# Moving the weight sums of down's last chunk and the second group's dots on VectorE, in an octonion FFN with attention shortcut

## The chip, the cores and the metric

The kernel runs on one core of a Trainium2 chip. The metric is the device time of one execution in microseconds (us); lower is better. A core has engines with queues of their own: TensorE (PE in the profile, its weight loads PEld), VectorE (DVE), ScalarE (ACT), GpSimd (POOL), and SyncE (SP), which here only issues DMAs. Each engine runs its queue in order and meets the others through semaphores.

## The reference, cut to what matters

```python
x = L0_attn_x                                   # (1, 2048, 1024), f32
xn = _layernorm(x, axis=-1)
x = x + _L0_attn_ref(xn) + _L0_ffn_ref(xn, w_gate, w_up, w_down)

# _L0_attn_ref: autocorrelation of each row by FFT, its 6 largest lags, softmax, weighted sum of shifted rows
# _L0_ffn_ref, eight components i, j, k of an octonion, S its +-1 product table:
scale = jnp.mean(jnp.abs(W))
Wq = scale * jnp.clip(jnp.round(W / scale), -1.0, 1.0)      # ternary weights
M = jnp.einsum('jik,jod->koid', S_OCT, Wq)
linear(xp, W) = jnp.einsum('...id,koid->...ko', xp, M)
h = silu(linear(xp, w_gate)) * linear(xp, w_up)             # hidden: 8 x 341 or so
out = linear(hp, w_down)
```

The kernel replaces the attention part by the normalised row itself as long as a bound shows that lag zero has all of the softmax's weight. For that bound it needs of each row the spectrum and one number, the dot product of the row's first half with its second. A flag sends rows for which the bound fails to a slow path, which isn't taken here.

## The kernel before, in words

The 2048 rows go in eight groups of 256 (G = 8, two tiles t of 128 rows each). The hidden width of a component (341 units) is cut into three chunks c. For each group there are units of work, each with a bank pair of the accumulator in PSUM: X (transposes of the normalised rows), F (spectrum for the bound), G and U (gate and up of one chunk and one parity Y), L and H (the narrow third chunk, gate and up together), N (down, one tile of rows).

The octonion product is done by a fast form: sums and differences of components on the inputs ("hx" to "hs" and "hop" for the hidden values, x to "xop") and of the weights ("slots"), matmuls on these, and adds of quarters on VectorE behind them.

Who does what to the hidden values of a unit numbered m: ScalarE makes silu of the gate into hx; VectorE multiplies by up (`product`, L1540) and raises h_done; GpSimd waits for h_done, makes four sums (L1975, L1976, L1980, L1981, 128x512 f32, hs_done after each of the last two) and then two low halves (L1985, L1988); ScalarE makes the high halves (`h_high` L1015, `h_sums_high` L1025, which waits for the four sums); TensorE then uses hop for down.

The weights are prepared in the opening, T(m, c) for m = gate, up, down: TensorE transposes them, ScalarE takes signs (L900), VectorE makes the ternary values (`ternary`, L1349, two instructions) and the sums in `weight_slots` (two instructions L1366 and L1367 into a temporary, four more L1374 into the weights). For down the temporary, the ternary values (in zx) and the result wd are f16 in SBUF. GpSimd's sums read and write SBUF too.

The order on each engine is a list written out by hand. The opening ends on VectorE with `ternary(("T", 2, 1))`, `product(("U", 0, 1, 0))`, `weight_slots(("T", 2, 1))`, `out_scales()` (three tiny instructions, L1333 to L1335); second_group follows with `product(("U", 0, 1, 1))`, the adds of L(0,0,0), `least(("F", 1))`, the adds of L(0,0,1) and so on. ScalarE's list at the same place is

```python
            h_high(0, 1, 0)                 # end of the opening
            power(("F", 1))                 # L964, waits for TensorE's spectrum
            h_sums_high(0, 1, 0)            # L1025, waits for GpSimd's four sums of U(0, 1, 0)
            odd_two(("L", 0, 0, 0))         # L947
            eights(("T", 1, 0))             # L928
            refine(2)                       # L842 to L854
            odd_two(("L", 0, 0, 1))         # L947
```

`odd_two` copies half of a unit's sums out of PSUM, and VectorE's `first_adds` (L1423 to L1427) and `second_adds` (L1453 to L1459) of the same unit need that copy. TensorE's order in this stretch: direct products of U(0,1,1), spectrum F(1), first half of L(0,0,0), lags of F(1), first halves of L(0,0,1), L(0,1,0) and L(1,0,1), second half of L(0,0,0), then the second half of L(0,0,1), which waits for the end of that unit's `second_adds`.

A `dot(g, t)` is one VectorE instruction (L1382, 128x512 f32, both inputs in SBUF) with a read of the accumulator. For the second group (g = 1) both stand behind `x_sums_low(("X", 1, 0))`. SyncE's `load_x(2)` overwrites the rows in xr and waits for both dots and for the transposes of X(1,1). Its loads of zx wait for the last `weight_slots`, whose input lies in the same room.

Of the kernel before, what the change touches and what calls it, by code (L numbers as in the profile page):

```python
def octonion_ffn_attention_kernel(nc, x, w_gate, w_up, w_down, dft, lag, out):
# [19 lines left out]
    T = 256  # L21
    NT = T // P
# [94 lines left out]

    place = {u: n for n, u in enumerate(units)}
    bank = [b for _, b in opening] + [(n - OPEN + 3) % 4 for n in range(OPEN, N)]

    owner = {u: ([units[i] for i in range(n - 1, -1, -1) if bank[i] == bank[n] and units[i][0] != "-"] + [None])[0] for n, u in enumerate(units)}

    def is_direct(u):
        return u[0] in "GU" and u[1] == 0 and u[2] < DIRECTS
# [14 lines left out]
    def hidden(u):  # L139
        return (u[1], u[2], u[3]) if u[0] in "GU" else (u[1], 2, u[2])  # L140
# [20 lines left out]
    for u in units:  # L161
        if u[0] in "UH" and hidden(u)[0:2] not in halves and hidden(u)[0:2] != (G - 1, 1):
            two = sorted(spare[:2])
            spare = spare[2:]
            halves[hidden(u)[0:2]] = tuple(i for i, _ in two)
            free_after[hidden(u)[0:2]] = [n for _, n in two if n]
        if u[0] == "N":
            spare += [(halves[u[1], c][u[2]], u) for c in range(NC) if (u[1], c) in halves]
# [7 lines left out]
    with ctx:  # L176
# [76 lines left out]
        def bank_pair(n, rows=P):  # L253
            return acc[0:rows, bank[n], :, :]
# [26 lines left out]
        def slots(m, c):  # L281
            return (wg, wu)[m][:, c, :, :] if c < 2 else wl[:, :, m, 0:REST]
# [1020 lines left out]
        def _(dve):  # L1303
# [9 lines left out]
            def thresholds(m, u):  # L1313
                dve.wait_ge(total_mm, m + 1)
                nc.vector.tensor_reduce(tot[:, m:m + 1], acc[:, bank[place[u]], 0, 0:4], AX.X, ALU.add).then_inc(total_read, 1)
                dve.wait_ge(total_read, m + 1)
                nc.vector.tensor_scalar_mul(thr[:, m:m + 1], tot[:, m:m + 1], 0.5 / N_W).then_inc(thr_done[m], 1)
                dve.wait_ge(thr_done[m], 1)
# [13 lines left out]
            def out_scales():  # L1332
                link(nc.vector.tensor_scalar(osc[:, :], thr[:, 0:1], thr[:, 1:2], 2.0 / HS, ALU.mult, ALU.mult))  # L1333
                link(nc.vector.tensor_tensor(osc[:, :], osc[:, :], thr[:, 2:3], ALU.mult))
                link(nc.vector.tensor_scalar_mul(nosc[:, :], osc[:, :], -1.0))  # L1335

            def weights_of(u):

                _, m, c = u
                rows, cols = (P, WIDE[c]) if m < 2 else (WIDE[c], DB)  # L1340
                return rows, cols, slots(m, c)[:, 2 * NJ:3 * NJ, :] if m < 2 else wt[t_no[u] % 2][0:rows, :, 0:cols]

            def ternary(u):
                _, m, c = u
                k, n = t_no[u], place[u]
                rows, cols, val = weights_of(u)
                for b in range(2):
                    dve.wait_ge(sign_done, 2 * k + b + 1)
                    nc.vector.scalar_tensor_tensor(val[:, 4 * b:4 * b + 4, :],  # L1349
                                                   acc[0:rows, bank[n], b, :].rearrange("p (j d) -> p j d", j=4)[:, :, 0:cols],  # L1350
                                                   thr[0:rows, m:m + 1], wt[k % 2][0:rows, 4 * b:4 * b + 4, 0:cols], ALU.is_gt, ALU.min).then_inc(tern_done, 1)

            def weight_slots(u):
                _, m, c = u
                i = slots_no[u]
                rows, cols, val = weights_of(u)
                dve.wait_ge(tern_done, 2 * t_no[u] + 2)
                two = val.rearrange("p (b i v) d -> p b i v d", b=2, i=2)
                s = tt[i % 2][0:rows, :, :, 0:cols]
                if u == ("T", 1, 0):  # L1360

                    dve.wait_ge(first_slots, 1)
                if u == ("T", 2, 1):

                    dve.wait_ge(term_mm, prod_no["G", 0, 1, 1] + 1)
                nc.vector.tensor_tensor(s[:, 0:3:2, :, :], two[:, :, 0, :, :], two[:, :, 1, :, :], ALU.add)  # L1366
                nc.vector.tensor_tensor(s[:, 1:4:2, :, :], two[:, :, 0, :, :], two[:, :, 1, :, :], ALU.subtract).then_inc(pairs_done, 1)  # L1367
                dve.wait_ge(pairs_done, i + 1)
                for op, (a, alu) in enumerate(((0, ALU.add), (0, ALU.subtract), (1, ALU.add), (1, ALU.subtract))):
                    if m < 2:  # L1370
                        dst = slots(m, c)[:, 4 * op:4 * op + 4, :].rearrange("p (b v) d -> p b v d", b=2)
                    else:
                        dst = wd[0:rows, 4 * op:4 * op + 4, c, :].rearrange("p (b v) d -> p b v d", b=2)
                    last = nc.vector.tensor_tensor(dst, s[:, a:a + 1, :, :].broadcast_to([rows, 2, 2, cols]), s[:, 2:4, :, :], alu)  # L1374
                last.then_inc(slots_done, 1)

            def dot(g, t):
                k = NT * g + t
                dve.wait_ge(norm_done, NT * g + NT)
                if k:  # L1380
                    dve.wait_ge(dot_done, k)
                nc.vector.scalar_tensor_tensor(dj[:, :], xr[:, t, 0:D // 2], 1.0, xr[:, t, D // 2:D], ALU.mult, ALU.mult,  # L1382
                                               accum_out=dots[:, k:k + 1]).then_inc(dot_done, 1)
# [133 lines left out]
            def x_low(u):  # L1517
                four = bank_pair(place[u]).rearrange("p b (i t) -> p (b i) t", t=T)
                at = 4 * u[2]
                dve.wait_ge(xhi_done, x_no[u] + 1)  # L1520
                nc.vector.scalar_tensor_tensor(xop[:, u[1] % 2, at:at + 4, 1, :], four, XS, xop[:, u[1] % 2, at:at + 4, 0, :], ALU.mult, ALU.subtract).then_inc(xlo_done, 1)

            def x_adds(u):
                first_adds(u)
                if u[2] == 1:
                    fold_sum(u)
                second_adds(u)

            def x_sums_low(u):
                at = NJ + 4 * u[2]  # L1530
                dve.wait_ge(xhs_done, x_no[u] + 1)
                nc.vector.tensor_tensor(xop[:, u[1] % 2, at:at + 4, 1, :], bank_pair(place[u]).rearrange("p b (i t) -> p (b i) t", t=T),
                                        xop[:, u[1] % 2, at:at + 4, 0, :], ALU.subtract).then_inc(x_ready, 1)

            def product(u):
                m = h_no[hidden(u)]
                dve.wait_ge(term_mm, prod_no[u] + 1)
                dve.wait_ge(silu_done, g_no["G", *u[1:]] + 1)
                scale = ((hsc4, nhsc4) if is_direct(u) else (hsc, nhsc))[u[3]]
                nc.vector.scalar_tensor_tensor(hx[:, m % 4, :, :], hx[:, m % 4, :, :], scale[:, :],  # L1540
                                               bank_pair(place[u]).rearrange("p b (i t) -> p (b i) t", t=T), ALU.mult, ALU.mult).then_inc(h_done, 1)
# [6 lines left out]
            def least(u):  # L1548
                dve.wait_ge(lag_mm, f_no[u] + 1)
                nc.vector.tensor_reduce(dmin[:, NT * u[1]:NT * u[1] + NT], acc[:, bank[place[u]], 1, :].rearrange("p (t l) -> p t l", t=NT),  # L1550
                                        AX.X, ALU.min).then_inc(bound_done, 1)
# [59 lines left out]
            x_sums_low(("X", 0, 0))  # L1611
            x_sums_low(("X", 0, 1))
            dot(0, 0)
            dot(0, 1)
            thresholds(1, ("U", 0, 0, 0))
            ternary(("T", 1, 0))
# [8 lines left out]
            weight_slots(("T", 0, 1))  # L1625
            least(("F", 0))
            thresholds(2, ("F", 0))
            ternary(("T", 1, 1))
            product(("U", 0, 0, 1))
            x_low(("X", 1, 0))  # L1630
            x_adds(("X", 1, 0))
            ternary(("T", 2, 2))
            x_sums_low(("X", 1, 0))
            dot(1, 0)
            dot(1, 1)
            x_low(("X", 1, 1))
            x_adds(("X", 1, 1))
            ternary(("T", 2, 0))
# [3 lines left out]
            weight_slots(("T", 2, 2))  # L1642
            weight_slots(("T", 2, 0))
            ternary(("T", 2, 1))
            product(("U", 0, 1, 0))
            weight_slots(("T", 2, 1))
            out_scales()

            def second_group():
# [374 lines left out]
```

## Time and profile before

| | |
|---|---|
| median of 3 runs | 553.96 us (553.83 to 554.98) |
| profiled execution, its own time | 553.78 us |
| its span in the trace | 552.0 us |
| TensorE busy | 539.7 us (98%) |
| VectorE busy | 472.3 us (86%) |
| ScalarE busy | 385.0 us (70%) |
| GpSimd busy | 466.7 us (85%) |
| TensorE's granted clock | 1.00 of full speed, in every slice |

The span starts with the first instruction in the trace; 1.78 us of the profiled execution lie outside it. A matmul's end is modelled, so busy time says whether TensorE had work in hand and not how well it was used. Time zero in all the rows is the start of the span.

### The profile page before, as it was taken

The numbers are of one execution on the slowest core, as the hardware profiler recorded it, in microseconds if no ns is written. First come the engines' busy times: TensorE is split into PE (matmuls) and PEld (weight loads), VectorE is DVE, ScalarE is ACT, GpSimd is POOL, SyncE is SP. The second block draws the span as 40 slices with busy tenths as digits, with TensorE's granted clock in tenths as the row PEclk, the third lists the DMA queues.
The fourth block names the chain that finished last, engine by engine and source line by source line (L and its number), as shares of the span: only waits on it lengthen the run. The fifth ranks groups of instructions, "written<-read, shape, count | busy, mean of one in ns | idle before, by whom it ended". The sixth has DMA issues, their size and how long they took to land.

```text
span 552.0 us, 16462 instructions
## 1 busy us (share of the span) xinstructions
PE 539.7 (98%) x6596; PEld 507.2 (92%) x6596; DVE 472.3 (86%) x1227; ACT 385.0 (70%) x622; POOL 466.7 (85%) x337
## 2 busy tenths in 40 slices
PE   6999999999999999999999999999999999999997
PEld 5899998899998999999999999999999999998997
DVE  4987999898888879988998979987998979984965
ACT  4879889976947589665977589766967575646432
POOL 3506739998999998999989998999989999999950
PEclk9999999999999999999999999999999999999999
DMA  9820212013220042201330042201330021302122
GB/s 207 193 78 1 77 27 82 8 38 110 79 88 17 3 153 66 66 1 39 137 100 12 1 152 67 65 4 44 130 99 12 3 77 35 95 3 71 33 87 97
DMA packets 26996, 36.65 MB, mean 66 GB/s; under 512 B 13686, under 2 KB 20774, under 8 KB 26918
## 3 DMA queue, kind: packets, MB, share of 16 engines
q1 hardware_dynamic: 26918, 35.58, 21.8%
q8 instruction: 52, 0.85, 0.6%
q14 instruction: 26, 0.21, 0.1%
HBM read 21.23 MB, written 8.39 MB: 54 GB/s over the span
## 4 chain that ended last, share of the span: by engine, by line
PE 70%; POOL 13%; issue 9%; DVE 4%; DMA 2%; ACT 2%; SPq 0%; POOLq 0%; ACTq 0%; DVEq 0%
PE acc L659 17%; PE acc L495 14%; PE acc L488 13%; PE acc L505 10%; PE acc L649 6%; PE acc L544 4%; POOL hop L1988 3%; POOL hs L1981 3%; POOL hs L1976 3%; POOL hs L1980 3%; PE acc L518 2%; DMA hop<-in_w_gate 2%; PE acc L561 2%; POOL hop L1985 1%; POOL hs L1975 1%
## 5 line engine op out<-in xcount | busy, mean ns | idle before, releaser
L659 PE MATMUL acc<-wd,hop 128*128 128x128 f16 x1920 | 112.7, 219 | 0.8 <-DVE acc L1441 0.4
L659 PEld LDWEIGHTS acc<-wd,hop 128*128 128x128 f16 x1920 | 109.4, 98 | 1.7 <-DVE acc L1441 0.9
L947 ACT ACTIVATE pk<-acc 128x512 f32<-128x512 f32 (+1 forms) x120 | 65.9, 556 | 64.0 <-PE acc L488 26.2
L1988 POOL TENSOR_TENSOR hop<-hs,hop 128x1024 f16<-128x1024 f32 (+1 forms) x46 | 98.2, 2135 | 9.0 <-ACT hop L1025 8.8
L1985 POOL TENSOR_TENSOR hop<-hx,hop 128x1024 f16<-128x1024 f32 (+1 forms) x46 | 98.3, 2137 | 5.3 <-ACT hop L1015 5.3
L505 PE MATMUL acc<-wl,xop 128*128 128x172 f16 x1024 | 84.2, 237 | 1.1 <-DVE acc L1459 0.9
L505 PEld LDWEIGHTS acc<-wl,xop 128*128 128x128 f16 x1024 | 77.6, 97 | 3.2 <-DVE acc L1459 1.1
L1975 POOL TENSOR_TENSOR hs<-hx 128x512 f32<-128x512 f32 (+1 forms) x47 | 60.2, 1281 | 15.3 <-DVE hx L1540 11.7
L1423 DVE TENSOR_TENSOR bd<-acc,pk 128x256 f32<-128x256 f32 (+1 forms) x104 | 41.0, 394 | 30.0 <-ACT pk L947 29.6
L1025 ACT ACTIVATE hop<-hs 128x1024 f16<-128x1024 f32 (+1 forms) x46 | 48.4, 1053 | 23.8 <-POOL hs L1981 23.7
L1980 POOL TENSOR_TENSOR hs<-hs 128x512 f32<-128x512 f32 (+1 forms) x47 | 59.8, 1273 | 3.7
L1981 POOL TENSOR_TENSOR hs<-hs 128x512 f32<-128x512 f32 (+1 forms) x47 | 60.4, 1285 | 0.0
L1976 POOL TENSOR_TENSOR hs<-hx 128x512 f32<-128x512 f32 (+1 forms) x47 | 60.0, 1277 | 0.0
L495 PE MATMUL acc<-xop,wu 128*128 128x256 f16 x448 | 53.3, 273 | 0.0
L488 PE MATMUL acc<-xop,wg 128*128 128x256 f16 x448 | 53.3, 273 | 0.0
L1015 ACT ACTIVATE hop<-hx 128x1024 f16<-128x1024 f32 (+1 forms) x46 | 48.5, 1055 | 6.8 <-DVE hx L1540 3.5
L488 PE MATMUL acc<-xop,wu 128*128 128x256 f16 x448 | 52.3, 273 | 0.5 <-ACT hx L979 0.5
L495 PE MATMUL acc<-xop,wg 128*128 128x256 f16 x448 | 52.7, 273 | 0.0
L488 PEld LDWEIGHTS acc<-xop,wu 128*128 128x128 f16 x448 | 43.6, 98 | 5.6 <-ACT hx L979 0.8
L649 PE MATMUL acc<-wd,hop 85*128 85x128 f16 (+2 forms) x720 | 48.5, 219 | 0.0
L488 PEld LDWEIGHTS acc<-xop,wg 128*128 128x128 f16 x448 | 43.7, 98 | 4.9
L495 PEld LDWEIGHTS acc<-xop,wg 128*128 128x128 f16 x448 | 43.3, 98 | 4.8
(206 smaller groups left out, 1164.2 us busy)
## 6 DMA issues: line engine op xcount, KB each, us to landing
xr<-in_x SPq DMA_DIRECT2D x16, 512.0 KB, 4.4
zx<-in_x SPq DMA_DIRECT2D x16, 512.0 KB, 3.6
out_y<-zx SPq DMA_DIRECT2D x15, 512.0 KB, 2.6
hop<-hop SPq DMA_DIRECT2D x40, 84.0 KB
hop<-hop SPq DMA_DIRECT2D x96, 21.0 KB
hop<-in_w_gate SPq DMA_DIRECT2D x2, 480.0 KB, 9.6
hop<-in_w_up SPq DMA_DIRECT2D x1, 960.0 KB
hop<-in_w_down SPq DMA_DIRECT2D x1, 960.0 KB, 17.3
```

The costliest lines, as they stand in the source:

```text
L488: last = nc.tensor.matmul(acc[:, bank[n], s // 2, T * (s % 2):T * (s % 2 + 1)], wm[:, c, slot, :], xop[:, g % 2, form, level, :], start=s ...
L495: last = nc.tensor.matmul(acc[:, bank[n], s // 2, T * (s % 2):T * (s % 2 + 1)], wm[:, c, slot, :], xop[:, g % 2, form, level, :], start=Fa ...
L505: last = nc.tensor.matmul(acc[:, bank[n], s // 2, T * (s % 2):T * (s % 2) + PAIR], xop[:, g % 2, form, level, P * t:P * (t + 1)], wl[:, sl ...
L649: last = nc.tensor.matmul(dst, lhs, rhs, start=which == 0 and c == order[0] and s // 2 not in seen, stop=part == 2 and c == order[-1] and ...
L659: last = nc.tensor.matmul(dst, operand(g, c, t, form, level), wd[0:WIDE[c], slot, c, :], start=which == 0 and c == order[0] and s // 2 not ...
L947: nc.scalar.activation(pk[:, q % 2, :, 0:wide], pair[:, :, T:T + wide], ACT.Copy, scale=XS if u[0] == "X" else 1.0).then_inc(copied, 1)
L1975: nc.gpsimd.tensor_tensor(hs[rows, 4:8:2, :], h[:, 0:4:2, :], h[:, 1:4:2, :], ALU.add)
L1976: nc.gpsimd.tensor_tensor(hs[rows, 5:8:2, :], h[:, 0:4:2, :], h[:, 1:4:2, :], ALU.subtract).then_inc(hpair_done, 1)
L1980: nc.gpsimd.tensor_tensor(hs[rows, 0:2, :], hs[rows, 4:6, :], hs[rows, 6:8, :], ALU.add).then_inc(hs_done, 1)
L1981: nc.gpsimd.tensor_tensor(hs[rows, 2:4, :], hs[rows, 4:6, :], hs[rows, 6:8, :], ALU.subtract).then_inc(hs_done, 1)
L1985: nc.gpsimd.tensor_tensor(half_of(g, c, 4 * Y, 1), by_tile(h), half_of(g, c, 4 * Y, 0), ALU.subtract).then_inc(h_free, 1)
L1988: nc.gpsimd.tensor_tensor(half_of(g, c, NJ + 4 * Y, 1), by_tile(hs[rows, 0:4, :]), half_of(g, c, NJ + 4 * Y, 0), ALU.subtract).then_inc(h_ ...
```

## The change

It moves four calls in VectorE's list and loosens one wait. `dot(1, 0)` goes up behind `thresholds(2, ...)`, `dot(1, 1)` behind `product(("U", 0, 0, 1))`. A dot now waits for the normalised tile that it reads and, in the first group as before, for both. `weight_slots(("T", 2, 1))` changes places with `product(("U", 0, 1, 0))`. Nothing is added or taken away.

```diff
             def dot(g, t):
                 k = NT * g + t
-                dve.wait_ge(norm_done, NT * g + NT)
+                dve.wait_ge(norm_done, max(k + 1, NT))
...
             thresholds(2, ("F", 0))
+            dot(1, 0)
             ternary(("T", 1, 1))
             product(("U", 0, 0, 1))
+            dot(1, 1)
             x_low(("X", 1, 0))
             x_adds(("X", 1, 0))
             ternary(("T", 2, 2))
             x_sums_low(("X", 1, 0))
-            dot(1, 0)
-            dot(1, 1)
             x_low(("X", 1, 1))
...
             ternary(("T", 2, 1))
+            weight_slots(("T", 2, 1))
             product(("U", 0, 1, 0))
-            weight_slots(("T", 2, 1))
             out_scales()
```

## Rows read from the trace of the kernel before

**Rows 1.** The page, busy time of each engine.

```profile
PE 539.7 (98%) x6596; PEld 507.2 (92%) x6596; DVE 472.3 (86%) x1227; ACT 385.0 (70%) x622; POOL 466.7 (85%) x337
```

**Rows 2.** Waits of TensorE over the whole span: total us, times, longest.

```profile
PE acc L505 <- DVE acc L1459: 0.9, 1, 0.9
...
PE acc L488 <- ACT hx L979: 0.5, 1, 0.5
```

**Rows 3.** Timeline of TensorE: start us, us, what, idle before and releaser.

```profile
59.76 2.35 PE L544 MATMUL acc<-xop,wg 128*128 128x256 f16 x20
...
81.25 1.47 PE L544 MATMUL acc<-xop,junk 128*128 128x256 f16 x12
...
90.59 4.00 PE L505 MATMUL acc<-wl,xop 128*128 128x172 f16 x48 [0.89 <-DVE acc L1459]
```

**Rows 4.** Timeline of ScalarE around the moved steps.

```profile
45.80 2.36 ACT L859 ACTIVATE xr<-xr,nmrs,rs 128x1024 f32<-128x1024 f32 x2
...
60.72 1.03 ACT L954 ACTIVATE xop<-acc 128x1024 f16<-128x1024 f32 x1
...
83.19 0.60 ACT L964 ACTIVATE pw<-acc 128x512 f16<-128x512 f32 x1 [2.05 <-PE acc L574]
83.69 1.05 ACT L1025 ACTIVATE hop<-hs 128x1024 f16<-128x1024 f32 x1
...
88.02 0.77 ACT L947 ACTIVATE pk<-acc 128x344 f32<-128x344 f32 x2
```

**Rows 5.** Timeline of VectorE, the last chunk of down and what follows.

```profile
72.66 0.41 DVE L1366 TENSOR_TENSOR zx<-zx 128x512 f16<-128x512 f16 x1
...
74.79 1.41 DVE L1349 SCALAR_TENSOR_TENSOR zx<-acc,few,zx 128x512 f16<-128x512 f32 x2
76.11 1.27 DVE L1540 SCALAR_TENSOR_TENSOR hx<-hx,few,acc 128x1024 f32<-128x1024 f32 x1
...
78.09 5.61 DVE L1374 TENSOR_TENSOR wd<-zx 128x512 f16<-128x512 f16 x4
...
84.24 1.28 DVE L1540 SCALAR_TENSOR_TENSOR hx<-hx,few,acc 128x1024 f32<-128x1024 f32 x1
...
88.49 0.34 DVE L1423 TENSOR_TENSOR bd<-acc,pk 128x172 f32<-128x172 f32 x1 [0.40 <-ACT pk L947]
```

**Rows 6.** Timeline of GpSimd: sums of three hidden units.

```profile
46.38 1.27 POOL L1975 TENSOR_TENSOR hs<-hx 128x512 f32<-128x512 f32 x1 [3.66 <-DVE wg L1374]
...
51.43 2.13 POOL L1985 TENSOR_TENSOR hop<-hx,hop 128x1024 f16<-128x1024 f32 x1
...
77.46 1.72 POOL L1975 TENSOR_TENSOR hs<-hx 128x512 f32<-128x512 f32 x1 [10.44 <-DVE hx L1540]
...
81.97 1.44 POOL L1981 TENSOR_TENSOR hs<-hs 128x512 f32<-128x512 f32 x1
...
88.41 1.27 POOL L1975 TENSOR_TENSOR hs<-hx 128x512 f32<-128x512 f32 x1
...
92.21 1.28 POOL L1981 TENSOR_TENSOR hs<-hs 128x512 f32<-128x512 f32 x1
```

**Rows 7.** Timeline of VectorE earlier in the opening, where the dots stand.

```profile
42.56 1.41 DVE L1349 SCALAR_TENSOR_TENSOR wg<-acc,few,zx 128x512 f16<-128x512 f32 x2 [0.75 <-ACT zx L900]
44.01 0.42 DVE L1366 TENSOR_TENSOR zx<-wg 128x512 f16<-128x512 f16 x1
...
48.83 1.41 DVE L1349 SCALAR_TENSOR_TENSOR wu<-acc,few,zx 128x512 f16<-128x512 f32 x2 [1.72 <-ACT zx L900]
...
52.76 1.22 DVE L1521 SCALAR_TENSOR_TENSOR xop<-acc,xop 128x1024 f16<-128x1024 f32 x1 [1.20 <-ACT xop L954]
...
58.99 1.24 DVE L1382 SCALAR_TENSOR_TENSOR dj<-xr 128x512 f16<-128x512 f32 x1
...
61.84 1.21 DVE L1521 SCALAR_TENSOR_TENSOR xop<-acc,xop 128x1024 f16<-128x1024 f32 x1
```

**Rows 8.** SyncE's queue: issue of the loads of zx.

```profile
84.35 1.82 SPq L376 DMA_DIRECT2D zx<-in_x  x2
```

## The prediction, made before the change was run

> **What bounds the kernel now.** I read the page first: TensorE has work in 539.7 us of a span of 552.0, VectorE and GpSimd in some 85% [rows 1]. So time can only come from, or go into, the 12.3 us in which TensorE stands still. Its waits say where these are: most lie in the first 28 us and at the end. Between 28 us and 160 us there is one wait of note, 0.9 us at 90.59, for VectorE's last add of unit L(0,0,1); the next, 0.5 us, comes at 168 us for a silu [rows 2, 3]. Everything the change touches is in front of the wait at 90.59. Then I followed that wait back through the timelines. VectorE began the adds of L(0,0,1) at 88.49 after 0.40 us idle for ScalarE's copy [rows 5]. That copy, at 88.02, is the end of a run of ScalarE work without a pause that began with power at 83.19, where ScalarE had waited 2.05 us for TensorE's spectrum, and whose second piece is h_sums_high at 83.69 [rows 4]. h_sums_high needs GpSimd's four sums, which ended at 81.97 + 1.44 = 83.41 [rows 6]. The slack is 83.69 - 83.41 = 0.28 us. This number decides: GpSimd's sums of U(0,1,0) are nearly late already.
>
> The chain of waits itself runs along GpSimd here, which had stood idle 10.44 us until VectorE's product let it begin at 77.46 [rows 6].
>
> **The change part by part.** First the swap. Before, the six instructions of the last weight_slots ran beside GpSimd's sums: the four L1374 took 5.61 us, and product to next product is 84.24 - 76.11 = 8.13 us [rows 5]. The same six without GpSimd, for chunk T(2,0), took 74.79 - 72.66 = 2.13 us [rows 5]. GpSimd paid too: from the start of its four sums to their end was 83.41 - 77.46 = 5.95 us, against 92.21 + 1.28 - 88.41 = 5.08 us undisturbed [rows 6].
>
> In the new order the slots run before GpSimd has anything to do, in 2.13 us. One more term: they need the ternary values just written. Ternary to slots was 44.01 - 42.56 = 1.45 us in another chunk, ternary to product 76.11 - 74.79 = 1.32 us, so 0.13 us is added [rows 5, 7]. The product moves from 76.11 to 76.11 + 2.13 + 0.13 = 78.37, less the 0.06 us that I give the dots below: 78.31. GpSimd followed the product's start by 77.46 - 76.11 = 1.35 us [rows 5, 6], so it begins at 79.66 and ends its four sums at 79.66 + 5.08 = 84.74. VectorE then only has tiny scales to do beside it.
>
> What hangs on it: ScalarE has done power by about 83.7 and waits for the sums, as it never did here before. With 0.04 us for the handover (in the row above product to GpSimd it is 77.46 - (76.11 + 1.27) = 0.08, so 0.04 to 0.08), h_sums_high starts at about 84.78 instead of 83.69: 1.09 us late. Behind it in ScalarE's queue stand the copy of L(0,0,0), eights, refine and the copy of L(0,0,1); they had no pause between them, so each is 1.09 us late too. VectorE's adds of L(0,0,1) then start at 89.58, and TensorE's second half of that unit at 91.68: its wait grows from 0.9 to 2.0 us. The shorter waits that open earlier (least F(1) and the adds of L(0,0,0), some 0.6 us late each) lie inside the same 2.0 us.
>
> VectorE itself gains: its next product was at 84.24. It would be free at about 80.1, but that product needs TensorE's U(0,1,1), which ends at 81.25 + 1.47 = 82.72 [rows 3]. So it starts at about 82.8, 1.4 us sooner, and then waits for ScalarE. The 4.2 us saved on VectorE end in waits.
>
> After 91.7 us all engines are late alike: TensorE has work without pause, GpSimd goes on 1.06 to 1.09 us late, and I find no later wait for something that isn't itself late (the wait of 0.5 us at 168 us is behind GpSimd and ScalarE work of the same pipeline). So 1.09 us reaches the end.
>
> Second, the dots. Behind x_sums_low they ran from 58.99 to 61.84, 2.85 us for two, beside GpSimd. The next step, x_low of X(1,1), needs ScalarE's high half, which ended at 60.72 + 1.03 = 61.75 [rows 4, 7]. So taking the dots away lets VectorE go on 0.06 us sooner, and the rest becomes a pause: the dots were hidden. dot(1,0) comes into a pause of 1.72 us ending at 48.83; VectorE is free at 47.11, and the first of two normalisations ends at about 45.80 + 1.2 = 47.0 [rows 4, 7]. At 1.43 us or less it fits. dot(1,1) comes into the pause of 1.20 us from 51.56 to 52.76 [rows 7]. Alone it takes less than beside GpSimd, where both ends count: nothing late if it gets in as GpSimd's fourth sum ends at about 51.4 to 51.9, over 1.5 us late if it must sit out the L1985 of 2.13 us [rows 6]. I take nothing: dot(1,0) delays GpSimd's second sum by about 1.72 - 1.27 = 0.45 us, so the fourth sum is still running when dot(1,1) is issued, and L1985 is not yet.
>
> The queues passed: both dots feed SyncE's load of the third group's rows, which can be issued up to 2 us sooner (not before TensorE's transposes at 59.76) and which nobody waited for. The loads of zx wait for the slots, which end at 78.3 instead of 83.7; but SyncE issued them at 84.35 straight behind its other weight copies [rows 8], so they stay. Worth nothing. h_high of U(0,1,0) came at 80.1, behind other ScalarE work, and the later product at 79.6 doesn't hold it up.
>
> Weighed against the skill: that slots and GpSimd's sums hold each other up is seen at 5.61 us for four L1374 alone, where all six instructions took 2.13 us without GpSimd [rows 5]. The Trainium skill (page "SBUF — State Buffer", section "Who interferes with whom") says that a VectorE instruction with two SBUF inputs contends with a GpSimd instruction that reads SBUF, and that the first to issue has the port for its whole instruction. By it, a change that ends such an overlap pays on both engines; the trace agrees (8.13 us, and 5.95 against 5.08), yet the sum by the rows is a loss, since the overlap held up nothing that TensorE waited for. The same rule would make dot(1,1) the loser if L1985 starts first, the third rival.
>
> **Sum.** Against the profiled execution: 553.78 + 1.09 = 554.87. Its own range is +0.8 us (no drain of 0.13, GpSimd a little quicker) to +1.4 us (a slower handover, a scale instruction in GpSimd's way). The profiled execution is 0.18 us below the median, so on the median's scale 553.96 + 1.09 = 555.05; I say 555.0.
>
> **Rivals.** (a) Faster: VectorE's head start is what counts, and the wait of 0.9 us shrinks. For: that wait names VectorE, and VectorE is saved 4.2 us. Against: VectorE stood idle 0.40 us for ScalarE's copy just before. It decides if h_sums_high isn't later than 83.7, that is if GpSimd's sums end 1.05 us sooner than I reckon, and the copies then come sooner as well. All 0.9 us gone: 553.96 - 0.9 = 553.1. Chance 0.11.
>
> (b) No effect: the lateness is taken up, by GpSimd's quicker sums or by the wait of 0.5 us at 168 us being for something that is not late. Left 0 to 0.6 us: 553.96 to 554.6, middle 554.2. Against: 168 us lies behind 70 us of TensorE work without a pause. Chance 0.17.
>
> (c) Slower by more: dot(1,1) loses against L1985. It would end at about 51.9 + 2.1 + 0.6 = 54.6, and x_low be some 1.8 us late. x_sums_low of X(1,0), which ended at about 59.1 [rows 7], then ends at 60.9, and TensorE, which takes that bank at 59.76 [rows 3], waits 1.1 us. X(1,1)'s high half on ScalarE comes 0.5 us late, with it the product, GpSimd's sums and h_sums_high: 1.09 + 0.5 = 1.6 us, 555.55. For: the margin is 0.4 us of GpSimd's time. Chance 0.15.
>
> The forecast has the remaining 0.57.
>
> **The numbers.** 0.2% is 1.1 us, about what a measurement of this kernel can tell from no change, and my forecast lies on that line. Slower by over 0.2%: all of (c) and some 0.27 of the forecast's 0.57, 0.42. Within 0.2%: (b) and the other 0.30, 0.47. Faster: (a), 0.11. The range leaves out most of (a), and reaches from (b)'s lower end, 553.8, to a little above (c), 555.8.
>
> **What would show it.** Right: the six instructions of the last chunk's slots take about 2.1 us; GpSimd's idle time before the sums of U(0,1,0) grows from 10.4 to some 12.5 us and the four take 5.1; h_sums_high on ScalarE shows a wait of about 1 us for GpSimd's L1981; TensorE's wait before its second half of L(0,0,1) is about 2.0 us; VectorE idles some 2.7 us before x_low of X(1,1). Wrong: TensorE's wait at 90.6 is unchanged or smaller; a new TensorE wait near 60 us, which is (c); or all the later work catches up by 168 us.

## The result, and the profile after

Beside the kernel before on the same chips, the changed kernel took 555.75 us (median of 21 runs, 554.92 to 558.18) and the kernel before 554.67 us (21 runs, 553.83 to 556.25). The ratio is 1.0023, with a 95% interval of 1.0014 to 1.0031: slower by 1.28 us (0.8 to 1.7). The median of before was 553.96 us when I predicted, from three runs; with 21 it is 0.7 us higher. The two medians differ by 555.75 - 554.67 = 1.08 us; the ratio of times gives a little more, and both lie in the interval. The profiled execution of the change took 555.75 us, its span is 554.0.

The page, busy time of each engine after the change [rows 1 before]:

```profile
PE 541.3 (98%) x6596; PEld 508.4 (92%) x6596; DVE 468.5 (85%) x1227; ACT 385.2 (70%) x622; POOL 466.2 (84%) x337
```

VectorE is busy 3.8 us less and GpSimd 0.5 us less, and the kernel is slower: what the overlap cost these two isn't what the kernel is bound by.

Timeline of TensorE after, the counterparts of [rows 3] and what follows:

```profile
60.50 2.35 PE L544 MATMUL acc<-xop,wg 128*128 128x256 f16 x20
...
81.98 1.47 PE L544 MATMUL acc<-xop,junk 128*128 128x256 f16 x12
...
88.68 2.55 PE L505 MATMUL acc<-wl,xop 128*128 128x172 f16 x32 [0.78 <-DVE dmin L1550]
92.44 1.36 PE L505 MATMUL acc<-wl,xop 128*128 128x172 f16 x16 [1.21 <-DVE acc L1459]
93.97 2.56 PE L505 MATMUL acc<-wl,xop 128*128 128x172 f16 x32 [0.17 <-DVE hx L1546]
```

Whatever doesn't wait for the moved work is 0.73 us later here than in the profile of before: 81.98 against 81.25. Nearly all of that (0.65 us) was there before 18 us, ahead of anything that the change touches (the first weights and the first transposes); the other runs have between -0.39 and +0.54 us of it. It has to be taken off before two times are compared. Then TensorE's waits are 0.78 + 1.21 = 1.99 us where [rows 3] has 0.89, and the second half of L(0,0,1) starts 92.44 - 90.59 - 0.73 = 1.12 us late.

Timeline of ScalarE after, as in [rows 4]:

```profile
83.93 0.60 ACT L964 ACTIVATE pw<-acc 128x512 f16<-128x512 f32 x1 [2.10 <-PE acc L574]
85.53 1.06 ACT L1025 ACTIVATE hop<-hs 128x1024 f16<-128x1024 f32 x1 [1.00 <-POOL hs L1981]
...
89.87 0.78 ACT L947 ACTIVATE pk<-acc 128x344 f32<-128x344 f32 x2
```

Timeline of GpSimd after, as in [rows 6]:

```profile
52.62 2.58 POOL L1985 TENSOR_TENSOR hop<-hx,hop 128x1024 f16<-128x1024 f32 x1
...
80.42 1.27 POOL L1975 TENSOR_TENSOR hs<-hx 128x512 f32<-128x512 f32 x1 [12.66 <-DVE hx L1540]
...
84.21 1.28 POOL L1981 TENSOR_TENSOR hs<-hs 128x512 f32<-128x512 f32 x1
```

Timeline of VectorE after, as in [rows 5] and [rows 7]:

```profile
47.88 1.06 DVE L1382 SCALAR_TENSOR_TENSOR dj<-xr 128x512 f16<-128x512 f32 x1
...
52.21 1.00 DVE L1382 SCALAR_TENSOR_TENSOR dj<-xr 128x512 f16<-128x512 f32 x1
...
53.49 1.23 DVE L1521 SCALAR_TENSOR_TENSOR xop<-acc,xop 128x1024 f16<-128x1024 f32 x1 [0.27 <-ACT xop L954]
...
62.53 1.23 DVE L1521 SCALAR_TENSOR_TENSOR xop<-acc,xop 128x1024 f16<-128x1024 f32 x1 [2.72 <-ACT xop L954]
...
76.93 0.42 DVE L1366 TENSOR_TENSOR zx<-zx 128x512 f16<-128x512 f16 x1
...
77.72 1.43 DVE L1374 TENSOR_TENSOR wd<-zx 128x512 f16<-128x512 f16 x4
79.07 1.27 DVE L1540 SCALAR_TENSOR_TENSOR hx<-hx,few,acc 128x1024 f32<-128x1024 f32 x1
...
80.50 1.20 DVE L1334 TENSOR_TENSOR few<-few 128x1 f32<-128x1 f32 x1
81.74 0.15 DVE L1335 TENSOR_SCALAR few<-few 128x1 f32<-128x1 f32 x1
...
83.55 1.28 DVE L1540 SCALAR_TENSOR_TENSOR hx<-hx,few,acc 128x1024 f32<-128x1024 f32 x1 [1.65 <-PE acc L544]
...
90.33 0.34 DVE L1423 TENSOR_TENSOR bd<-acc,pk 128x172 f32<-128x172 f32 x1 [0.73 <-ACT pk L947]
```

Read from the bottom up, the chain is the predicted one. VectorE waits for ScalarE's copy (now 0.73 us, before 0.40), the copy stands behind h_sums_high, and that waited 1.00 us for GpSimd's last sum, with no wait before. GpSimd stood idle 12.66 us instead of 10.44 and then took 85.49 - 80.42 = 5.07 us for its four sums instead of 5.95.

### The profile page after: what moved, and what is told of

The parts are those of the page before. It is cut to its first block, busy times and chain, and to the rows that moved or that the text cites. A ratio compares the mean times of both kernels' runs of the same rounds, so it can differ in the third digit from the quotient of the medians.

```text
span 554.0 us, 16461 instructions
## 1 busy us (share of the span) xinstructions
PE 541.3 (98%) x6596; PEld 508.4 (92%) x6596; DVE 468.5 (85%) x1227; ACT 385.2 (70%) x622; POOL 466.2 (84%) x337
## 4 chain that ended last, share of the span: by engine, by line
PE 69%; POOL 13%; issue 9%; DVE 4%; DMA 2%; ACT 2%; SPq 0%; POOLq 0%; ACTq 0%; DVEq 0%
PE acc L659 17%; PE acc L495 14%; PE acc L488 13%; PE acc L505 10%; PE acc L649 6%; PE acc L544 4%; POOL hop L1988 3%; POOL hs L1976 3%; POOL hs L1980 3%; POOL hs L1981 2%; PE acc L518 2%; DMA hop<-in_w_gate 2%; PE acc L561 2%; POOL hop L1985 1%; POOL hs L1975 1%
## 5 line engine op out<-in xcount | busy, mean ns | idle before, releaser
L1985 POOL TENSOR_TENSOR hop<-hx,hop 128x1024 f16<-128x1024 f32 (+1 forms) x46 | 98.8, 2147 | 5.1 <-ACT hop L1015 5.0
L1975 POOL TENSOR_TENSOR hs<-hx 128x512 f32<-128x512 f32 (+1 forms) x47 | 60.0, 1276 | 17.5 <-DVE hx L1540 13.9
L1976 POOL TENSOR_TENSOR hs<-hx 128x512 f32<-128x512 f32 (+1 forms) x47 | 60.4, 1286 | 0.0
L1981 POOL TENSOR_TENSOR hs<-hs 128x512 f32<-128x512 f32 (+1 forms) x47 | 59.9, 1276 | 0.0
```

Source lines behind the costliest of these rows:

```text
L1975: nc.gpsimd.tensor_tensor(hs[rows, 4:8:2, :], h[:, 0:4:2, :], h[:, 1:4:2, :], ALU.add)
L1976: nc.gpsimd.tensor_tensor(hs[rows, 5:8:2, :], h[:, 0:4:2, :], h[:, 1:4:2, :], ALU.subtract).then_inc(hpair_done, 1)
L1981: nc.gpsimd.tensor_tensor(hs[rows, 2:4, :], hs[rows, 4:6, :], hs[rows, 6:8, :], ALU.subtract).then_inc(hs_done, 1)
L1985: nc.gpsimd.tensor_tensor(half_of(g, c, 4 * Y, 1), by_tile(h), half_of(g, c, 4 * Y, 0), ALU.subtract).then_inc(h_free, 1)
```

## A ruler that leaves the scatter out

Single executions of one kernel spread over 1 to 3 us, more than the effect. So beside each ratio I read one length from TensorE's timeline: from the start of the transposes of X(1,1) to that of X(2,0), 58.89 to 115.10 us in the profile of before. It contains the swap and all that follows from it up to there. The dots' new places lie ahead of it, and cost nothing there: from the transposes of X(1,0) to those of X(1,1) it is 58.89 - 50.08 = 8.81 us before and 59.62 - 50.81 = 8.81 us after. For the kernel before it is 56.21, 56.20 and 56.21 us in three executions. The two profiled executions of before and of the change differ by 555.75 - 553.78 = 1.97 us: 0.73 is the opening, 1.20 this length, and 0.04 the rest.

| kernel | length, us | against before | ratio of times (95%) |
|---|---|---|---|
| before | 56.21, 56.20, 56.21 | | |
| the change | 57.41 | +1.20 | 1.0023 (1.0014 to 1.0031) |
| e1 swap only | 57.38 | +1.17 | 1.0015 (1.0002 to 1.0027) |
| e2, e10 dots only | 56.29, 56.30 | +0.08, +0.09 | 1.0006 (0.9995 to 1.0018), 0.9996 (0.9985 to 1.0007) |
| e7 before, GpSimd one sum more | 57.39 | +1.18 | 1.0021 (1.0011 to 1.0032) |
| e8 change, GpSimd one sum less | 56.29 | +0.08 | 0.9998 (0.9988 to 1.0009) |
| e3 change, copies first | 58.91 | +2.70 | 1.0033 (1.0019 to 1.0047) |
| e4 before, copies first | 57.68 | +1.47 | 1.0061 (1.0038 to 1.0084) |
| e5 change, three copies sooner | 55.74 | -0.47 | 0.9996 (0.9985 to 1.0007) |
| e6 before, three copies sooner | 55.74 | -0.47 | 0.9987 (0.9976 to 0.9998) |
| e9 as e6, scales later | 55.72 | -0.49 | 0.9995 (0.9985 to 1.0006) |

## The experiments

**e1, the swap alone.**

```diff
             ternary(("T", 2, 1))
+            weight_slots(("T", 2, 1))
             product(("U", 0, 1, 0))
-            weight_slots(("T", 2, 1))
             out_scales()
```

> Only the last weight_slots changes places with the product; the dots stay where they were. Theory (GpSimd's sums of U(0,1,0) end too late for ScalarE, whose queue stands in h_sums_high): all of the loss is here, 1.0 to 1.3 us slower than before, ratio about 1.002; ScalarE waits about 1.0 us for GpSimd's L1981 and TensorE's waits between 85 and 94 us sum to about 2.1 us instead of 0.9. Rival (the dots beside GpSimd, or the earlier load, cost something): less than half of the loss, under 0.5 us.

The ruler gives +1.17 us, nearly all of the change. TensorE's and ScalarE's timelines of e1:

```profile
87.97 2.55 PE L505 MATMUL acc<-wl,xop 128*128 128x172 f16 x32 [0.84 <-DVE dmin L1550]
91.73 4.00 PE L505 MATMUL acc<-wl,xop 128*128 128x172 f16 x48 [1.21 <-DVE acc L1459]
```

```profile
84.81 1.06 ACT L1025 ACTIVATE hop<-hs 128x1024 f16<-128x1024 f32 x1 [1.05 <-POOL hs L1981]
```

The waits are 2.05 us together, ScalarE's wait 1.05. The loss is the swap's.

**e2 and e10, the dots alone**, twice: the diff of the change without its last hunk.

> Only the dots move; the last weight_slots stays behind the product. Theory: nothing, within 0.2 us of before; VectorE shows a pause of 2.7 us before x_low of X(1,1), ScalarE's h_sums_high has no wait, TensorE waits 0.9 us before the second half of L(0,0,1) as before. Rival (the dots cost it): 0.5 to 1.2 us slower.

> The dots alone a second time, because 1.0006 with an interval of 0.9995 to 1.0018 left 0 and the missing 0.2 us both open. Theory: 0, so a ratio of 0.9995 to 1.0005. Rival: the dots cost 0.3 us or more.

One row of TensorE's timeline of e2:

```profile
91.14 1.36 PE L505 MATMUL acc<-wl,xop 128*128 128x172 f16 x16 [0.94 <-DVE acc L1459]
```

VectorE's timeline at the same place, of before and then of e2:

```profile
90.20 0.34 DVE L1459 SCALAR_TENSOR_TENSOR acc<-acc,bd 128x172 f32<-128x172 f32 x1
90.45 0.33 DVE L1423 TENSOR_TENSOR bd<-acc,pk 128x172 f32<-128x172 f32 x1
```

```profile
90.75 0.33 DVE L1459 SCALAR_TENSOR_TENSOR acc<-acc,bd 128x172 f32<-128x172 f32 x1
91.06 0.34 DVE L1423 TENSOR_TENSOR bd<-acc,pk 128x172 f32<-128x172 f32 x1
```

The wait is that of before, and the two ratios lie on both sides of 1. On the ruler the dots cost 0.08 and 0.09 us. All kernels that move the dots and nothing in ScalarE's list (the change, e2, e10, e8) show a wait of 0.16 or 0.17 us for a left product right behind L(0,0,1), which before, e1 and e7 don't have. The rows show where it comes from: behind its last add of L(0,0,1), VectorE starts the adds of the next unit, L(0,1,0), 0.31 us later in e2 and 0.25 us later in before, and the left product stands behind these adds. It is 0.31 or 0.32 us in all six kernels with the dots moved and 0.24 or 0.25 us in all the others. Why the dots' places matter to this step, some 40 us later, the traces don't tell.

**e7, GpSimd late and nothing else.** The kernel before, with one more sum on GpSimd into a room of its own.

```diff
+                if (g, c, Y) == (0, 1, 0):
+                    nc.gpsimd.tensor_tensor(spare_sum[rows, :, :], h[:, 0:4:2, :], h[:, 1:4:2, :], ALU.add)
                 nc.gpsimd.tensor_tensor(hs[rows, 4:8:2, :], h[:, 0:4:2, :], h[:, 1:4:2, :], ALU.add)
```

> The kernel before with nothing moved, but GpSimd makes one more sum of 128x512 into a room of its own ahead of the four of U(0,1,0), which delays the four by 1.3 to 1.7 us. It separates GpSimd's lateness from everything else in the change. Theory: 0.28 us is slack, the rest shows at TensorE's wait before the second half of L(0,0,1): 1.0 to 1.4 us slower than before, with ScalarE waiting about that long for L1981. Rival (the loss needs the moved slots or product): no loss, or a loss at another place.

Timelines of e7, TensorE, ScalarE and VectorE (its lines are one or a few higher for the same code, so that L1981 is L1984 here):

```profile
86.60 1.37 PE L506 MATMUL acc<-wl,xop 128*128 128x172 f16 x16 [0.45 <-DVE hx L1541]
88.21 2.55 PE L506 MATMUL acc<-wl,xop 128*128 128x172 f16 x32 [0.24 <-DVE dmin L1551]
91.97 4.00 PE L506 MATMUL acc<-wl,xop 128*128 128x172 f16 x48 [1.21 <-DVE acc L1460]
```

```profile
85.05 1.06 ACT L1026 ACTIVATE hop<-hs 128x1024 f16<-128x1024 f32 x1 [1.08 <-POOL hs L1984]
```

```profile
84.05 0.98 DVE L1335 TENSOR_TENSOR few<-few 128x1 f32<-128x1 f32 x1
```

Nothing on VectorE was moved, and the loss is the same: +1.18 us, ratio 1.0021, ScalarE waits 1.08 us for the same sum. GpSimd's lateness is enough by itself. The first wait, 0.45 us, is new: VectorE's tiny instruction took 0.98 us beside a GpSimd sum, which held up the next product. It added nothing to the loss: the second half of L(0,0,1) starts 91.97 - 90.59 - 0.19 = 1.19 us late (0.19 us is e7's opening), as late as in e1 (1.18), which has no such wait.

**e8, the change with GpSimd on time.** One of the four sums is left out for this unit, so part of down's input is wrong.

```diff
+                if (g, c, Y) != (0, 1, 0):
                     nc.gpsimd.tensor_tensor(hs[rows, 4:8:2, :], h[:, 0:4:2, :], h[:, 1:4:2, :], ALU.add)
```

> The whole change with one of GpSimd's four sums of U(0,1,0) left out (L1975, so that hs keeps the sums of an earlier unit there and the output is not the reference's): the four end 1.2 us sooner, at about 83.5 us. Theory: ScalarE doesn't wait, TensorE's wait at 90.6 is 0.9 us again, and the loss is gone: within 0.2 us of before. Rival (a): even 0.5 to 0.9 us faster than before, since VectorE has its head start and GpSimd is on time. If instead about 1 us stays lost, GpSimd's sums are not the cause.

Timelines of e8, TensorE, ScalarE and VectorE:

```profile
90.56 1.36 PE L505 MATMUL acc<-wl,xop 128*128 128x172 f16 x16 [1.06 <-DVE acc L1459]
```

```profile
83.65 1.05 ACT L1025 ACTIVATE hop<-hs 128x1024 f16<-128x1024 f32 x1
```

```profile
82.78 1.28 DVE L1540 SCALAR_TENSOR_TENSOR hx<-hx,few,acc 128x1024 f32<-128x1024 f32 x1 [1.64 <-PE acc L544]
...
88.45 0.34 DVE L1423 TENSOR_TENSOR bd<-acc,pk 128x172 f32<-128x172 f32 x1 [0.72 <-ACT pk L947]
```

The loss is gone: +0.08 us, what the dots cost, and 0.9998. ScalarE has no wait for GpSimd. TensorE's wait reads 1.06 us and not the expected 0.9, but it ends where it did before, at 90.56 with an opening 0.04 us earlier than that of before. So GpSimd's lateness is necessary too. And my rival (a) falls with it: here VectorE has its whole head start (1.64 us of waiting for TensorE, 0.72 for the copy) and GpSimd is on time, and nothing is gained.

**e3 and e4, the copies freed, first try.** In ScalarE's list:

```diff
                 power(("F", 1))
-                h_sums_high(0, 1, 0)
                 odd_two(("L", 0, 0, 0))
-                eights(("T", 1, 0))
-                refine(2)
+                h_sums_high(0, 1, 0)
                 odd_two(("L", 0, 0, 1))
                 odd_two(("L", 0, 1, 0))
+                eights(("T", 1, 0))
                 odd_two(("L", 1, 0, 1))
                 left_silu(("L", 0, 0, 0))
                 h_high(0, 1, 1)
-                eights(("T", 0, 0))
                 left_silu(("L", 0, 0, 1))
+                refine(2)
+                eights(("T", 0, 0))
                 normalise(2, 0)
```

> The whole change, and in ScalarE's list the copies of L(0,0,0), L(0,0,1) and L(0,1,0) no longer stand behind h_sums_high, eights and refine. Theory: with what waits for GpSimd out of the way of the copies, both the added wait of 1.2 us and the old one of 0.9 us go, so 0.5 to 0.9 us faster than the kernel before, and about 2 us faster than the change alone; GpSimd's sums start as late as in the change. Rival (it is GpSimd's lateness itself that reaches the end, through down's operands): stays 1.0 us or more slower than before, with the wait moved to a later place.

> The kernel before with the same order of ScalarE's list. VectorE then begins the adds of L(0,0,1) at about 88.1 us, straight behind those of L(0,0,0), so by the theory TensorE's wait shrinks from 0.9 to about 0.5 us: 0.4 us faster than before. Beside e3 it tells what the swap is worth once ScalarE doesn't stand in front of it: e3 should be about 0.4 us faster than this one. If the head start of VectorE is worth nothing even then, both are equal.

Both fell. The waits for L(0,0,1) went or shrank as expected, but a larger one came, in TensorE's timelines of e3 and then of e4:

```profile
98.24 3.95 PE L505 MATMUL acc<-wl,xop 128*128 128x172 f16 x32 [1.97 <-DVE hx L1546]
```

```profile
90.29 4.00 PE L505 MATMUL acc<-wl,xop 128*128 128x172 f16 x48 [0.38 <-DVE acc L1459]
...
98.54 2.55 PE L505 MATMUL acc<-wl,xop 128*128 128x172 f16 x32 [1.95 <-DVE hx L1546]
```

My order pushed refine into a stretch where ScalarE has no pause, ahead of the copy of L(0,1,1), which stands in front of the silu of L(0,1,0). VectorE waited 1.84 us for that copy in e4 and 1.86 us in e3, and its left product came late behind it: the same fault as the change's, made by hand. It also brought something that I come to below. Whether GpSimd's lateness also reaches down's operands, the rival of e3, isn't told by this pair.

**e5 and e6, a smaller edit.** Two calls are put back in ScalarE's list, h_sums_high by one place and refine by two, so that three copies come sooner.

```diff
                 power(("F", 1))
-                h_sums_high(0, 1, 0)
                 odd_two(("L", 0, 0, 0))
+                h_sums_high(0, 1, 0)
                 eights(("T", 1, 0))
-                refine(2)
                 odd_two(("L", 0, 0, 1))
                 odd_two(("L", 0, 1, 0))
+                refine(2)
                 odd_two(("L", 1, 0, 1))
```

> The whole change, with a smaller edit to ScalarE's list than the last: the copy of L(0,0,0) before h_sums_high, the copies of L(0,0,1) and L(0,1,0) before refine; everything from the copy of L(1,0,1) on keeps its order. ScalarE then reaches that copy at about 89.6 us, as in the kernel before, in spite of GpSimd's later sums. Theory: TensorE's waits between 84 and 92 us go (2.1 us in the change, 0.9 before), and no silu is put off as in the last order; 0.3 to 0.9 us faster than before. Rival (the time comes back as a wait for a silu or a left product near 94 us, ScalarE being full here): the same as before within 0.3 us, with a wait of about 0.5 to 1 us for a left product.

> The kernel before with the same edit of ScalarE's list. Theory: TensorE's wait before the second half of L(0,0,1) shrinks from 0.9 to 0.4 us, 0.2 to 0.5 us faster than before; the swap is worth some 0.4 us more beside it. Rival: as for the last one, no gain.

TensorE's timelines of e5, then of e6:

```profile
91.50 2.56 PE L505 MATMUL acc<-wl,xop 128*128 128x172 f16 x32 [0.21 <-DVE hx L1546]
94.25 1.07 PE L518 MATMUL acc<-ident,hx 128*86 128x128 f32 x8 [0.19 <-DVE hx L1546]
...
124.15 1.50 PE L649 MATMUL acc<-wd,hop 85*128 85x128 f16 x24 [0.45 <-DMA hop<-hop]
```

```profile
90.11 4.01 PE L505 MATMUL acc<-wl,xop 128*128 128x172 f16 x48 [0.38 <-DVE acc L1459]
```

With the copies out of the way, the change's loss of 1.20 us turns into a gain of 0.47 us on the ruler, and the kernel before gains the same 0.47: the swap is then worth nothing, where I had said 0.4 us. It costs nothing there either, though GpSimd's sums end 1.36 us late as in the change (1.35), so the lateness reached TensorE by way of ScalarE's queue. In time, e5's gain doesn't show: its ratio is 0.9996, with 1 in the interval. In e5 the wait of 0.9 us is gone, and ScalarE's silus and VectorE's left products take over (0.21 + 0.19 us). Past the ruler e5 also waited 0.45 us for the DMA of stacked operands at 124 us. That wait was 0.32 us in one profile of before, so it isn't shown that GpSimd's later sums cause it. e6 is a little faster than the kernel before, 0.9987 (0.9976 to 0.9998).

**e9, e6 with out_scales later**, ahead of the first output.

```diff
             weight_slots(("T", 2, 1))
-            out_scales()
...
                 x_low(("X", 2, 1))
+                out_scales()
                 output(("N", 0, 0))
```

> The kernel before with the two copies ahead of refine (the edit that measured 0.9987) and the three tiny scale instructions taken out of VectorE's way: they move from behind the last weight_slots to just ahead of the first output that needs them, where VectorE waited 1.3 us. If what is left of TensorE's wait (0.4 us at 90.1) is VectorE's own work, it shrinks by 0.4 us to nothing: 0.6 to 1.0 us faster than before. Rival (ScalarE or GpSimd is next in line at once, or the first output is late): no faster than the edit of the copies alone, 0.4 to 0.7 us.

TensorE's timeline of e9:

```profile
91.36 2.56 PE L505 MATMUL acc<-wl,xop 128*128 128x172 f16 x32 [0.20 <-DVE hx L1546]
94.11 1.07 PE L518 MATMUL acc<-ident,hx 128*86 128x128 f32 x8 [0.19 <-DVE hx L1546]
```

The last 0.38 us went, and 0.20 + 0.19 us stand in its place: the rival's case. 0.9995 and e6's 0.9987 can't be told apart; the ruler differs by 0.02 us.

**Two more profiles of the kernel before.**

> The kernel before itself, for its profile: whether TensorE's wait of 0.7 us for a silu in one of the middle groups, seen with the swap alone and with the dots alone but not in the first profile of before nor in that of the change, comes and goes from execution to execution. If it is chance it may show here too; if it belongs to the moved dots or slots it never does.

> The kernel before itself in a second execution, with the same question as the last run: does the 0.7 us wait for a silu in a middle group show without any edit?

TensorE's timeline of the first, then of the second:

```profile
90.97 4.00 PE L505 MATMUL acc<-wl,xop 128*128 128x172 f16 x48 [0.89 <-DVE acc L1459]
...
124.53 1.50 PE L649 MATMUL acc<-wd,hop 85*128 85x128 f16 x24 [0.32 <-DMA hop<-hop]
...
335.29 1.92 PE L488 MATMUL acc<-xop,wu 128*128 128x256 f16 x16 [0.56 <-ACT hx L977]
```

```profile
90.85 4.01 PE L505 MATMUL acc<-wl,xop 128*128 128x172 f16 x48 [0.89 <-DVE acc L1459]
```

The wait for a silu in a middle group shows without any edit, so the 0.67 us of it in e1 and 0.72 us in e2 say nothing of them. ScalarE's timeline of the first names its source, a row load that landed late:

```profile
332.93 1.06 ACT L795 ACTIVATE junk<-xr 128x1024 f16<-128x1024 f32 x1 [1.00 <-DMA xr<-in_x]
```

The wait at 90.6 us is 0.89 us in all three profiles of before.

## Why the prediction came out as it did

**The mechanism was right.** Slots alone in 2.1 us: 79.07 - 76.93 = 2.14. Product to GpSimd 1.35 us: 80.42 - 79.07 = 1.35. Four sums in 5.08 us: 5.07. h_sums_high late by 1.09 us: 85.53 - 83.69 - 0.73 = 1.11. In e1 the dots stay, so the 0.06 us that the prediction took off for them doesn't apply and its sum is 1.15; there, with an opening 0.04 us earlier than that of before, it is 84.81 - 83.69 + 0.04 = 1.16. TensorE's waits 2.0 us: 0.78 + 1.21 = 1.99. VectorE's next product started 1.4 us sooner and its head start ended in waits. The dots lay in pauses; dot(1,1) got in ahead of L1985, which took 2.58 us in place of 2.13, and 0.27 us of the pause was left. The loads of zx stayed where they were.

**The step that failed is one term of the sum, the dots, and what I made of the sum.** I had 1.09 us. The ruler shows 1.20 for the change. Up to h_sums_high the sum is short by 0.02 us, and the second half of L(0,0,1) starts 1.12 us late. The other 0.08 us come right behind it, as the wait of 0.17 us for a left product: the dots. I had priced their move at nothing beyond VectorE's 0.06 us head start; alone it measures +0.08 and +0.09 us (e2, e10). The ratio's 1.28 us agrees with 1.20 within its interval. Against a boundary of 1.1 us this 0.1 us decides the side: "within 0.2%", to which I gave the largest chance (0.47), was wrong, and "slower", 0.42, was right. It is a close call: the whole interval lies above 1, so the kernel is slower, but it reaches down to 0.14%, and the difference of the medians, 1.08 us, lies just below the line; the ratio and the ruler lie above it.

The forecast's 1.04 us (555.0 against 553.96) is four fifths of what was measured, and the time is inside the range, but I called it no change. Of the 0.47, 0.17 came from (b), for which no row spoke, and 0.30 from cutting the forecast's own case in two at a line on which it lay.

**The rivals.** (a) fell in e8. (b) fell: after the ruler the change follows before exactly, 332.50 us to the last group's X against 332.49. (c) didn't occur; TensorE had no wait near 60 us.

**The rule of the Trainium skill** (page "SBUF — State Buffer", section "Who interferes with whom"). That a VectorE instruction with two SBUF inputs contends with a GpSimd instruction that reads SBUF showed again in a place where I had seen no price. The scale instruction L1334, one element per partition with both inputs in SBUF, took 1.20 us beside GpSimd's L1975, while L1335, which has one such input, took 0.15 us beside L1976. In the profile of before L1334 took 0.16 us; GpSimd was in its tiny L1950 (128x2) then, which took 0.89 us against 0.72 in the change, so there it seems to be GpSimd that was held up; no run tests that. The long L1334 cost nothing in the change, for VectorE had to wait for TensorE anyway; in e7 it opened a wait of 0.45 us, which the loss doesn't contain.

What stays open: why moving the dots delays one start on VectorE by 0.07 us so much later, and whether GpSimd's lateness has any part in e5's wait for the stacked operands.

## What to carry to other kernels

Ending a collision between two engines pays only if one of the two was what the bound engine waited for. Look which of them hands over next, and how much slack that handover has: here VectorE had 3.8 us less to do, and GpSimd's sums, with 0.28 us of slack, ended 85.49 - 0.73 - 83.41 = 1.35 us later. In an ordered queue, an instruction that waits for a late engine holds up everything behind it that isn't late; the copies that VectorE and TensorE needed stood behind h_sums_high for no reason of data, and putting one copy ahead of it and two others ahead of refine gained 0.47 us on the ruler where the change lost 1.20. When executions scatter by more than the effect, measure a fixed length between two landmarks in the trace: it repeated to 0.01 us where times scattered by 2.

## What the runs showed of the hardware that I had not expected

In e3 TensorE's granted clock fell shortly after the wait of 1.97 us. The windows of e3 (length, busy time of each engine, PEclk, DMA share, GB/s):

```profile
96.00:98.00 2.00, 0.27 (x4) 0.06 (x1) 1.37 (x5) 2.00 (x5) 1.06 (x1) 1.00 0.00 0
98.00:100.00 2.00, 1.76 (x19) 1.77 (x20) 1.66 (x6) 2.00 (x4) 1.94 (x1) 0.79 0.00 0
100.00:102.00 2.00, 2.00 (x17) 2.00 (x15) 1.15 (x5) 0.76 (x2) 2.00 (x3) 0.50 0.00 0
102.00:104.00 2.00, 2.00 (x18) 1.69 (x16) 1.19 (x4) 1.68 (x2) 1.92 (x3) 0.86 0.00 0
```

0.50 is the lower of the two levels, 1.2 GHz; 32 matmuls of the narrow chunk took 3.95 us there against 2.55 in e4. So the stretch cost e3 more than the wait's length: +2.70 us on its ruler, where e4, whose wait was 1.95 us and whose profiled execution kept 1.00, has +1.47. A wait of that length is thus followed by a fall in one execution and not in another. Five of the seven executions of e4 had a mean clock of 0.997, as e3's profiled one has, and took 557.1 to 560.2 us, the other two 555.4 and 556.1 us. That goes some way to explain why e4's ratio, 1.0061, is far above what its ruler says, but two of the five took over 559 us, more than any execution of e3, and what they lost besides isn't known. The change itself, with two waits of 0.8 and 1.2 us, kept 1.00 in its profile.
